# A graph network with experts: joint norms in the first expert network, and a quad's sums cut to the nodes of each tile

## Chip, cores and metric

One core of a Trainium2 chip. The metric is the device time of the whole kernel in microseconds; TensorE, VectorE (DVE in the profile), ScalarE (ACT), GpSimd (POOL) and SyncE (SP, which here only issues transfers) work side by side and are ordered by semaphores.

## What is computed

The reference has 6250 nodes of 256 features and 206,250 edges, sorted by their destination. Everything is f32. Four stages, each added to its input `x`:

```python
# 1: first graph layer, 8 relations
msg = h[edge_src] * edge_norm[:, None]          # h = layernorm(x)
agg = segment_sum(msg, edge_rel * N + edge_dst)  # per relation and destination
out = einsum('rnbi,rbio->nbo', agg, W)           # block-diagonal weights
# 2: first expert network: 2 of 8 experts (512 hidden), the same two for all nodes
h = gelu(xf @ W1[e] + b1[e]); y = h @ W2[e] + b2[e]
out = layer_norm(sum_of_weighted_y + x, gamma, beta)
# 3: graph attention, 8 heads: softmax over the edges of each destination
# 4: second expert network, 8 experts of 256, gated per node
```

## The kernel before, in words

**First graph stage (`gnn0`, from 101 to 2112 us).** The edges lie in 1612 tiles of 128; four tiles are a quad (403 of them), 16 tiles a batch. POOL gathers the source rows of each tile by an indirect transfer (L840) into a ring of 64 tiles; it may run on when TensorE has summed the quad that lay there (`summed`). As edges are sorted, a quad touches few destinations: `NEAR` = 20 nodes from its first. VectorE makes a one-hot of each tile (`one_hots`, L1133) with 20 nodes times 8 relations = 160 columns, weighted by the edge; TensorE multiplies the gathered rows by it (`quad`, L1016), which sums the four tiles of a quad in one PSUM bank; each product is two instructions for each of the two feature halves. VectorE adds the bank to the cells of the batch (L1160), TensorE applies the relation weights (`weigh_one`, L999) and VectorE adds the window to the node sums (L1152). For the second graph stage the edges of the first 96 tiles are also counted by source and node (`pair_hots`, L1225, and `count`, L1056). Between, finished pairs of node tiles get their residual and norm (`norm`), and hidden layers of every second pair of the next network are computed ahead for all eight experts (`look_ahead`, L1067) and stored. `PARTS` says which of the 20 nodes each tile of a quad covers: before, all of them for all four. At the start, `edge_tables` derives from the data a flag, `k.narrow`, whether every tile lies within its part (L551 to L598); if not, all engines take a slower general path.

**First expert network (`ffn0`, 2128 to 2538 us).** 49 node tiles go in 25 pairs, the last of a single tile. `pair_steps` runs step s on every engine, each in its own program order, and a step works on several pairs:

- TensorE: the hidden layer of pair s (L1650; absent for even s below 20, whose hidden layer was computed ahead), interleaved with the output layer of pair s-1 (L1669, eight units of four instructions) and the projection of pair s-3 (L1692), one tile after output unit 0 and the other after unit 5; then the transposes of pair s-2 (`turn`, L1680).
- VectorE: the norm of pair s-2's output (`norm_output`: statistics L1415, aggregates L1419, variance L1421, inverse root by an integer guess and three Newton steps L194 to L199, then L1766 and L1773), `scores` of pair s-3's first tile (L1798 to L1801), the norm of the new rows of pair s-2 (`norm_rows`: statistics, aggregates and root again, then L1786), scores of the second tile, and the adds that take pair s-1's output from PSUM (`add`, L1758). The adds release TensorE's two output banks.
- POOL: waits for the finished rows (`row_done`) of pair s-3, then the residual of pair s (L1617, L1622) and beta of pair s-1 (L1628).
- SP: the ahead-computed hidden layer (L1576), the input of pair s+1 (L1551), and the stores of pair s-2's result (L1555) and pair s-3's table rows (L1564).
- ScalarE: gelu of each hidden unit (L1720), the copy of the transposes (L1726), the exponential for the scores (L1731).

Steps 0 to 3 are written out, 4 to 19 run in a loop, the rest is written out, up to step 27. The output bank of a projection is single: its second tile waits for the scores of the first (`p_moved`), its first for the scores of the second tile before.

**Second graph stage and network (`gnn1_ffn1`, from 2544 us).** It gathers rows of the table that `ffn0` stored (L2083) after a barrier; the change does not touch it.

## Time and profile before

| | |
|---|---|
| median of 3 runs | 4540.59 us (4539.41 to 4543.26) |
| profiled execution, its own time | 4537.89 us |
| its span, first to last instruction | 4535.9 us |
| mean granted TensorE clock | 0.918 of full |
| busy: TensorE, VectorE, ScalarE, POOL | 3594.7, 1875.2, 1064.4, 3081.6 us |
| gathers, first stage: first, last ends | 59.9, 2090.1 us |
| shift L194 beside POOL's add / alone | 1.07 / 0.17 us |
| two aggregates, L1419 | 0.25 us |

The span is what the trace covers, and times inside it count from its start. A profile line gives engine, source line, operation, written tile <- read tiles, count; in brackets the idle time of the engine before it and what ended it. A `PE` line is a matmul, `PEld` its weight load; overlapping instructions are counted once in busy time.

### The profile page before, as it was taken

To read this page: it belongs to the slowest core of one execution; us is meant where nothing else is said; L and a number is where in the kernel's file an instruction comes from. 1 tells how busy PE (TensorE), PEld (TensorE's weight loads), DVE (VectorE), ACT (ScalarE), POOL (GpSimd) and SP (SyncE) were. 2 spreads that over 40 slices of the span, in tenths; PEclk is the share of its full clock that TensorE was granted. 3 is DMA by queue.
4 is the path that set the end of the run, shared out by engine and by line. 5 is a ranking of instruction groups with operands and counts; after the bars stand their busy time and mean duration, and the time that the engine had idled before them with its cause. 6 is when DMAs were issued, how large, how long until landed. Compare 5 with 4: busy or idle time off the path is not lost. (4 is left out here: it accounts for less than half of the span.)

```text
span 4535.9 us, 68376 instructions
## 1 busy us (share of the span) xinstructions
PE 3594.7 (79%) x20702; PEld 3091.2 (68%) x20702; DVE 1875.2 (41%) x6475; ACT 1064.4 (23%) x2405; POOL 3081.6 (68%) x3233
## 2 busy tenths in 40 slices
PE   1777887888888888875889778888887878787788
PEld 1766777777777777774778666666666666666667
DVE  6644545455454544543777412222222222222222
ACT  3001111111111111111335112222222222222223
POOL 4777777777777777773222477777777777777771
PEclk7889999999998999997999888998899999999989
DMA  6344555555555555554221664444444444444441
GB/s 201 109 118 126 171 168 175 175 162 178 168 169 174 171 169 172 170 170 133 80 92 60 209 184 124 124 127 124 126 125 127 125 127 125 128 124 127 123 127 43
DMA packets 302410, 638.19 MB, mean 141 GB/s; under 512 B 66947, under 2 KB 142143, under 8 KB 302192
## 3 DMA queue, kind: packets, MB, share of 16 engines
q0 software_dynamic: 150672, 417.16, 32.6%
q1 hardware_dynamic: 80584, 142.91, 9.8%
q10 hardware_dynamic: 70936, 75.36, 5.1%
q8 instruction: 119, 1.95, 0.2%
q14 instruction: 99, 0.81, 0.1%
HBM read 534.13 MB, written 101.06 MB: 140 GB/s over the span
## 5 line engine op out<-in xcount | busy, mean ns | idle before, releaser
L840 POOL DMA_INDIRECT ring<-xn,index x1588 | 1505.1, 948 | 488.7 <-issue 474.0
L2083 POOL DMA_INDIRECT ring<-table,index x1516 | 1442.9, 952 | 483.4 <-issue 454.8
L1016 PE MATMUL bank<-spare,ring 128*128 128x160 f32 x6448 | 1196.5, 328 | 408.3 <-DMA ring<-xn,index 363.3
L1016 PEld LDWEIGHTS bank<-spare,ring 128*128 128x128 f32 x6448 | 1043.2, 211 | 475.3 <-issue 314.0
L1160 DVE TENSOR_TENSOR spare<-spare,bank 128x320 f32 x403 | 196.7, 488 | 957.4 <-PE bank L1016 932.2
L2405 PE MATMUL bank<-ring,acc 128*32 128x264 f32 x3032 | 292.4, 524 | 335.1 <-DMA ring<-table,index 333.6
L2184 ACT ACTIVATE ework<-bank,bn 128x256 f32<-128x256 f32 x800 | 407.8, 560 | 560.9 <-PE bank L2427 379.0
L1133 DVE TENSOR_SCALAR spare<-cell,scal 128x160 f32<-128x160 f32 x1612 | 510.9, 378 | 0.7 <-ACT scal L856 0.7
L905 ACT ACTIVATE fore_hid<-bank,fore_b 128x256 f32<-128x256 f32 x320 | 151.5, 473 | 1294.5 <-PE bank L1067 1169.8
L2405 PEld LDWEIGHTS bank<-ring,acc 128*32 128x32 f32 x3032 | 139.0, 140 | 451.3 <-issue 432.2
L2427 PE MATMUL bank<-acc,e_w 128*128 (+1 forms) x1600 | 397.4, 395 | 4.9 <-ACT acc L2175 1.7
L2605 DVE TENSOR_TENSOR acc<-cell,off 128x512 f32<-128x512 f32 x102 | 70.7, 693 | 753.2 <-PE bank L2415 729.4
L2440 PE MATMUL bank<-ework,e_w 128*128 128x256 f32 x1600 | 378.1, 379 | 0.0
L2452 PE MATMUL bank<-wo,ework 128*128 128x256 f32 x1600 | 377.9, 379 | 0.0
L2427 PEld LDWEIGHTS bank<-acc,e_w 128*128 128x128 f32 x1600 | 306.3, 197 | 98.3 <-issue 57.0
L1067 PE MATMUL bank<-acc,fore_w 128*128 x1280 | 344.0, 393 | 0.0
L2440 PEld LDWEIGHTS bank<-ework,e_w 128*128 128x128 f32 x1600 | 304.7, 190 | 42.0
L999 PE MATMUL bank<-spare,wblk 128*128 128x140 f32 x1632 | 330.4, 286 | 0.4 <-DVE spare L1160 0.4
L2452 PEld LDWEIGHTS bank<-wo,ework 128*128 128x128 f32 x1600 | 302.7, 190 | 39.5
L2680 DVE SCALAR_TENSOR_TENSOR y<-bank,gate,y 128x256 f32 (+1 forms) x400 | 175.0, 479 | 271.0 <-PE bank L2452 245.0
L999 PEld LDWEIGHTS bank<-spare,wblk 128*128 128x128 f32 x1632 | 270.2, 194 | 0.6 <-DVE spare L1160 0.6
L1067 PEld LDWEIGHTS bank<-acc,fore_w 128*128 128x128 f32 x1280 | 239.4, 203 | 19.2
(338 smaller groups left out, 3118.7 us busy)
## 6 DMA issues: line engine op xcount, KB each, us to landing
fore_w<-in_L_ffn_W SPq DMA_DIRECT2D x82, 512.0 KB, 5.7
fore<-fore_hid SPq DMA_DIRECT2D x80, 512.0 KB
ring<-xn,index POOLq DMA_INDIRECT x1612, 2.8
ring<-table,index POOLq DMA_INDIRECT x1516, 2.8
sums<-acc ACTq DMA_DIRECT2D x101, 132.0 KB, 2.2
hid<-fore SPq DMA_DIRECT2D x20, 512.0 KB, 4.5
counts<-panel ACTq DMA_DIRECT2D x72, 140.0 KB
table<-frow SPq DMA_DIRECT2D x24, 264.0 KB, 3.1
```

The source lines that it names most:

```text
L840: pool.indirect_dma_start(ring[:, m * BT + t, :], None, k.xn_d, bass.IndirectOffsetOnAxis(ap=index[m][:, t:t + 1], axis=0)).then_inc(got[m ...
L999: return pe.matmul(window_ps[:, h, :], k.wblk[:, h, r, :], cells[sums_of(m)][:, i, :], start=(r == 0), stop=(r == RELS - 1))
L1016: ins = pe.matmul(part_of(t, win[q][:, h, :]), ring[:, m * BT + q * QUAD + t, h * P:(h + 1) * P], part_of(t, onehot[:, (q * QUAD + t) % HE ...
L1067: ins = pe.matmul(fore_ps, fore_w[:, e % 2, h, c * P:(c + 1) * P], k.acc[:, h, cols(first_row(fore_group(a)), PCOLS)], start=(h == 0), sto ...
L1133: ins = dve.tensor_scalar(part_of(t % QUAD, onehot[:, t % HELD, :]), part_of(t % QUAD, k.cell[:]), scal[m][:, OFF_KIND, t:t + 1], scal[m][ ...
L1160: dve.tensor_tensor(here, here, win[q].rearrange("p h (r n) -> p (h r) n", n=NEAR), ALU.add).then_inc(added, 1)
L2083: pool.indirect_dma_start(ring[:, par * BT + t, :], None, k.table1_d, bass.IndirectOffsetOnAxis(ap=index[par][:, t:t + 1], axis=0)).then_i ...
L2184: ins = act.activation(dst[:, e % 2, c, :], src[e % 2][:, c, :], ACT.Relu, scale=bn[:, i, q:q + 1], bias=bn[:, i + 1, q:q + 1])
L2405: ins = pe.matmul(win[q * SLICE:(q + 1) * SLICE, :], onehot[:, par * BT + t, :], ring[:, tile_at(par, t), :], start=(u == 0), stop=(u == Q ...
L2427: ins = pe.matmul(p1[e % 2][:, c, :], wa[:, e, h, c * P:(c + 1) * P], xt[:, cols(j % 2 * H + h, 1), :].rearrange("p a n -> p (a n)"), star ...
L2440: ins = pe.matmul(p2[e % 2][:, c, :], wb[:, e, h, c * P:(c + 1) * P], h1[:, e % 2, h, :], start=(h == 0), stop=(h == CH - 1))
L2452: ins = pe.matmul(py[e % 2][:, t * D:(t + 1) * D], h2[:, e % 2, h, t * P:(t + 1) * P], wo[:, e, h, :], start=(h == 0), stop=(h == CH - 1))
```

## The change

`PARTS` becomes ((0, 8), (2, 12), (6, 16), (8, 20)): the four tiles of a quad cover nodes 0 to 7, 2 to 11, 6 to 15 and 8 to 19. All users of `PARTS` follow: one-hots and sums take 64, 80, 80 and 96 columns instead of 160, the counts 56, 70, 70 and 84 instead of 140 per group of blocks, and the flag's bounds are these. In `ffn0` one `statistics` call per step takes the statistics of pair s-2's output and of pair s-3's rows, with one aggregate, variance and root chain on up to four columns. Then come the scores of pair s-4, the row norm of pair s-3, the output norm of pair s-2, the other scores of pair s-4, and the adds of pair s-1. Transposes follow pair s-3, projections, exponentials and scores pair s-4, and one step more is run at the end. Steps 0 to 5 are written out instead of 0 to 3.

```diff
--- before.py
+++ after.py
@@ -74,7 +74,7 @@
 AHEAD0 = P - FIRST0
 NEAR = 20
 CELLS = NEAR * RELS
-PARTS = ((0, NEAR),) * QUAD
+PARTS = ((0, 8), (2, 12), (6, 16), (8, NEAR))
 WINDOW = 140
 PAIRED = 2 * QUADS
 CHUNK_X = 10
@@ -1446,14 +1446,14 @@
 
 
 
-    first, last = 4, 2 * FORE
+    first, last = 6, 2 * FORE
     assert first % 2 == 0 and last % 2 == 0 and last < PAIRS - 1
     for s in range(first):
         step(s, s % 2, s // 2)
     with eng.Fori(first // 2, last // 2) as i:
         step(2 * i, 0, i)
         step(2 * i + 1, 1, i)
-    for s in range(last, PAIRS + 3):
+    for s in range(last, PAIRS + 4):
         step(s, s % 2, s // 2)
 
 
@@ -1523,8 +1523,8 @@
         gamma, beta, b2 = (a.sb(n, [P, D]) for n in ("gamma", "beta", "b2_all"))
         wp = a.sb("wp", [P, H, ROW1])
         ln = Named()
-        ln.stats, ln.mv = a.sb("fstats", [P, PAIR, 6]), a.sb("fmv", [P, PAIR, 2])
-        ln.var, ln.rstd, ln.tmp = (a.sb(f"f{n}", [P, PAIR]) for n in ("var", "rstd", "tmp"))
+        ln.stats, ln.mv = a.sb("fstats", [P, 2 * PAIR, 6]), a.sb("fmv", [P, 2 * PAIR, 2])
+        ln.var, ln.rstd, ln.tmp = (a.sb(f"f{n}", [P, 2 * PAIR]) for n in ("var", "rstd", "tmp"))
         h_ps = [a.bank(f"fh_ps{i}", PCOLS) for i in range(BANKS)]
         y_ps = [a.bank(f"fy_ps{i}", D) for i in range(PAIR)]
         t_ps = a.bank("ft_ps", H * PAIR, P)
@@ -1584,8 +1584,8 @@
                     load(s + 1, 1 - par)
                 if is_pair(s - 2):
                     store_x2(s - 2, par)
-                if is_pair(s - 3):
-                    store_rows(s - 3, 1 - par)
+                if is_pair(s - 4):
+                    store_rows(s - 4, par)
                 if isinstance(s, int) and s == PAIRS - 2:
                     load_piece()
             _, which = nc.values_load_multi_w_load_instructions(
@@ -1629,8 +1629,8 @@
                                    ).then_inc(x1b_made, 1)
 
             def step(s, par, half):
-                if is_pair(s - 3):
-                    pool.wait_ge(row_done, PAIR * (s - 3) + tiles_of_pair(s - 3))
+                if is_pair(s - 4):
+                    pool.wait_ge(row_done, PAIR * (s - 4) + tiles_of_pair(s - 4))
                 if is_pair(s):
                     residual(s, par, half)
                 if is_pair(s - 1):
@@ -1706,10 +1706,10 @@
                         hidden(s, par, half, c)
                     if c >= LEAD and is_pair(s - 1):
                         output(s - 1, 1 - par, half - 1 + par, c - LEAD)
-                    if is_pair(s - 3) and ROWS_AT.get(c - LEAD, PAIR) < tiles_of_pair(s - 3):
-                        project(s - 3, ROWS_AT[c - LEAD])
-                if is_pair(s - 2):
-                    turn(s - 2)
+                    if is_pair(s - 4) and ROWS_AT.get(c - LEAD, PAIR) < tiles_of_pair(s - 4):
+                        project(s - 4, ROWS_AT[c - LEAD])
+                if is_pair(s - 3):
+                    turn(s - 3)
             pair_steps(pe, step)
 
         @block.scalar
@@ -1735,10 +1735,10 @@
                 for c in range(C + LEAD):
                     if c < C and is_pair(s) and not looked_ahead(s, par):
                         keep(s, par, half, c)
-                    if is_pair(s - 3) and ROWS_AT.get(c - LEAD, PAIR) < tiles_of_pair(s - 3):
-                        grow(s - 3, ROWS_AT[c - LEAD])
-                if is_pair(s - 2):
-                    keep_turned(s - 2)
+                    if is_pair(s - 4) and ROWS_AT.get(c - LEAD, PAIR) < tiles_of_pair(s - 4):
+                        grow(s - 4, ROWS_AT[c - LEAD])
+                if is_pair(s - 3):
+                    keep_turned(s - 3)
                 if isinstance(s, int) and s == 1:
                     act.wait_ge(b2_made, 1)
                     act.copy(b2[:], p_ps[:, 0:D]).then_inc(b2_kept, 1)
@@ -1748,8 +1748,7 @@
 
         @block.vector
         def _(dve):
-            HALF_STEPS = group_norm_steps(PAIR) + 2 * PAIR
-            NPER, RPER = HALF_STEPS + group_norm_steps(PAIR) + PAIR, 3
+            NORMS, RPER = group_norm_steps(2 * PAIR) + 3 * PAIR, 3
 
             def add(i, par, t):
                 if t == 0:
@@ -1757,11 +1756,35 @@
                 dve.wait_ge(y_made, PAIR * i + t + 1)
                 dve.tensor_tensor(y[:, t, :], y_ps[t], res[:, par, t, :], ALU.add).then_inc(y_added, 1)
 
-            def norm_output(i, par, half):
+            def statistics(st, o, r, par):
+                outs = [(t, y[:, t, :]) for t in range(tiles_of_pair(o))] if is_pair(o) else []
+                rows = [(PAIR + t, x2[:, 1 - par, t, :]) for t in range(tiles_of_pair(r))] if is_pair(r) else []
+                if outs:
+                    dve.wait_ge(y_added, PAIR * o + len(outs))
+                past_waits(dve, k)
+                for at, v in outs + rows:
+                    st.done(dve.bn_stats(ln.stats[:, at, :], v))
+                st.wait()
+                past_waits(dve, k)
+                for at, _ in outs + rows:
+                    st.done(dve.bn_aggr(ln.mv[:, at, :], ln.stats[:, at, :]))
+                st.wait()
+                used = slice(0 if outs else PAIR, (outs + rows)[-1][0] + 1)
+                st.then(dve.tensor_scalar(ln.var[:, used], ln.mv[:, used, 1], LN_EPS, None, ALU.add))
+                inverse_root(dve, st, ln.var[:, used], ln.rstd[:, used], ln.tmp[:, used])
+
+            def norm_rows(st, i, par):
+                if not (isinstance(i, int) and i == 0):
+                    dve.wait_ge(turned, i)
+                for t in range(tiles_of_pair(i)):
+                    at = PAIR + t
+                    st.done(dve.tensor_scalar(xn2[:, t, :], x2[:, par, t, :], ln.mv[:, at, 0:1], ln.rstd[:, at:at + 1],
+                                              ALU.subtract, ALU.mult))
+                st.wait()
+                dve.sem_inc(normed, 1)
+
+            def norm_output(st, i, par, half):
                 n = tiles_of_pair(i)
-                st = Steps(dve, steps, NPER * i, k)
-                dve.wait_ge(y_added, PAIR * i + n)
-                group_norms(dve, st, k, y, ln, [P] * n)
                 for t in range(n):
                     st.done(dve.scalar_tensor_tensor(y[:, t, :], y[:, t, :], ln.mv[:, t, 0:1], gamma[:],
                                                      ALU.subtract, ALU.mult))
@@ -1773,21 +1796,7 @@
                     st.done(dve.scalar_tensor_tensor(x2[:, par, t, :], y[:, t, :], ln.rstd[:, t:t + 1],
                                                      x1b[:, par, t, :], ALU.mult, ALU.add))
                 st.wait()
-                assert n < PAIR or st.n == HALF_STEPS
                 dve.sem_inc(x2_done, 1)
-
-            def norm_rows(i, par):
-                n = tiles_of_pair(i)
-                st = Steps(dve, steps, NPER * i + HALF_STEPS - 2 * (PAIR - n) * 2, k)
-                group_norms(dve, st, k, x2[:, par, :, :], ln, [P] * n)
-                if not (isinstance(i, int) and i == 0):
-                    dve.wait_ge(turned, i)
-                for t in range(n):
-                    st.done(dve.tensor_scalar(xn2[:, t, :], x2[:, par, t, :], ln.mv[:, t, 0:1], ln.rstd[:, t:t + 1],
-                                              ALU.subtract, ALU.mult))
-                st.wait()
-                assert n < PAIR or st.n == NPER - HALF_STEPS
-                dve.sem_inc(normed, 1)
 
             def scores(i, t, par, half):
 
@@ -1807,15 +1816,22 @@
                 dve.sem_inc(row_done, 1)
 
             def step(s, par, half):
-                tiles = tiles_of_pair(s - 3) if is_pair(s - 3) else 0
-                if is_pair(s - 2):
-                    norm_output(s - 2, par, half - 1)
+                o, r, q = s - 2, s - 3, s - 4
+                tiles = tiles_of_pair(q) if is_pair(q) else 0
+                st = Steps(dve, steps, NORMS * o, k)
+                if is_pair(o) or is_pair(r):
+                    statistics(st, o, r, par)
                 if tiles:
-                    scores(s - 3, 0, 1 - par, half - 2 + par)
-                if is_pair(s - 2):
-                    norm_rows(s - 2, par)
+                    scores(q, 0, par, half - 2)
+                if is_pair(r):
+                    norm_rows(st, r, 1 - par)
+                if is_pair(o):
+                    norm_output(st, o, par, half - 1)
+                if st.n and st.n < NORMS:
+                    dve.sem_inc(steps, NORMS - st.n)
+                assert st.n <= NORMS, st.n
                 if tiles > 1:
-                    scores(s - 3, 1, 1 - par, half - 2 + par)
+                    scores(q, 1, par, half - 2)
                 if is_pair(s - 1):
                     for t in range(tiles_of_pair(s - 1)):
                         add(s - 1, 1 - par, t)
```

## Rows read from the trace of the kernel before

**Rows 1.** The page's costliest groups: busy us, mean ns of one, idle before, releaser

```profile
L840 POOL DMA_INDIRECT ring<-xn,index x1588 | 1505.1, 948 | 488.7 <-issue 474.0
...
L2083 POOL DMA_INDIRECT ring<-table,index x1516 | 1442.9, 952 | 483.4 <-issue 454.8
```

**Rows 2.** Windows: stretch, length, busy us (instructions) by engine, clock, DMA share, GB/s

```profile
600.00:800.00 200.00, 164.93 (x1034) 153.24 (x1033) 103.33 (x369) 37.36 (x86) 151.24 (x161) 0.93 0.55 171
...
2352.00:2382.00 30.00, 26.07 (x123) 22.11 (x122) 23.95 (x93) 11.31 (x18) 7.06 (x6) 1.00 0.26 88
...
2472.00:2502.00 30.00, 30.00 (x158) 26.73 (x157) 21.98 (x88) 19.15 (x31) 7.07 (x6) 1.00 0.17 52
...
3400.00:3600.00 200.00, 160.73 (x925) 126.20 (x918) 51.93 (x160) 57.41 (x139) 151.25 (x161) 0.96 0.46 126
```

**Rows 3.** Waits, 400 to 1900 us: total us, times, longest us

```profile
POOL ring L840 <- PE bank L1016: 7.3, 24, 0.3
```

**Rows 4.** Timeline, first graph stage's tail: start us, us, engine, line, operation, idle before

```profile
2089.11 0.94 POOL L840 DMA_INDIRECT ring<-xn,index  x1 [0.30 <-issue]
...
2092.54 4.06 PE L1016 MATMUL bank<-spare,ring 128*128 128x160 f32 x16 [2.34 <-DMA ring<-xn,index]
...
2101.99 0.65 ACT L863 COPY nsums<-acc 128x512 f32<-128x512 f32 x1 [4.81 <-DVE acc L1152]
```

**Rows 5.** Timeline of the network, one step of VectorE

```profile
2281.53 0.76 DVE L1758 TENSOR_TENSOR fy<-fy_ps,fres 128x256 f32<-128x256 f32 x2 [0.42 <-DVE frow L1801]
...
2284.09 1.07 DVE L194 TENSOR_SCALAR ftmp<-fvar 128x2 int32<-128x2 int32 x1
...
2287.16 0.88 DVE L1766 SCALAR_TENSOR_TENSOR fy<-fy,fmv,gamma 128x256 f32<-128x256 f32 x2
...
2289.49 0.23 DVE L1798 TENSOR_SCALAR fraw<-fp_ps,fm 128x8 f32<-128x8 f32 x1 [0.34 <-DVE fx L1773]
...
2290.64 0.75 DVE L1415 BATCH_NORM_STATS2 fstats<-fx 128x6 f32<-128x256 f32 x2 [0.33 <-DVE frow L1801]
...
2294.31 0.74 DVE L1786 TENSOR_SCALAR fxn<-fx,fmv,frstd 128x256 f32<-128x256 f32 x2
...
2296.43 0.75 DVE L1758 TENSOR_TENSOR fy<-fy_ps,fres 128x256 f32<-128x256 f32 x2 [0.34 <-DVE frow L1801]
```

**Rows 6.** Timeline of the network, the same stretch, TensorE and POOL

```profile
2269.27 1.03 PE L1669 MATMUL fy_ps<-w,hid 128*128 128x256 f32 x4
...
2279.69 1.89 PE L1669 MATMUL fy_ps<-w,hid 128*128 128x256 f32 x8
...
2283.88 1.26 POOL L1628 TENSOR_TENSOR fx1b<-fx,beta 128x512 f32<-128x512 f32 x1
...
2290.42 1.52 PE L1692 MATMUL fp_ps<-wp,fxt 128*128 128x264 f32 x4 [1.99 <-DVEq L1805]
...
2291.73 3.26 PE L1669 MATMUL fy_ps<-w,hid 128*128 128x256 f32 x8
...
2295.65 3.62 PE L1650 MATMUL fh_ps<-acc,w 128*128 x16
```

**Rows 7.** Timeline of the network, its start, the ends of steps, its last store

```profile
2172.79 1.12 PE L1680 MATMUL ft_ps<-ident,fxn 128*128 128x128 f32 x4 [5.89 <-DVEq L1790]
...
2192.01 0.75 DVE L1758 TENSOR_TENSOR fy<-fy_ps,fres 128x256 f32<-128x256 f32 x2 [0.68 <-PE fy_ps L1669]
...
2430.70 0.76 DVE L1758 TENSOR_TENSOR fy<-fy_ps,fres 128x256 f32<-128x256 f32 x2 [0.42 <-DVE frow L1801]
...
2494.74 0.76 DVE L1758 TENSOR_TENSOR fy<-fy_ps,fres 128x256 f32<-128x256 f32 x2 [0.33 <-DVE frow L1801]
...
2509.21 0.76 DVE L1758 TENSOR_TENSOR fy<-fy_ps,fres 128x256 f32<-128x256 f32 x2 [0.32 <-DVE frow L1801]
...
2523.01 0.42 DVE L1758 TENSOR_TENSOR fy<-fy_ps,fres 128x256 f32<-128x256 f32 x1 [0.33 <-DVE frow L1801]
...
2537.66 0.31 SPq L1562 DMA_DIRECT2D table<-frow  x1
```

## The prediction

> **What bounds the kernel now.** I read the groups of instructions first, then the windows, the waits, and the timeline of three places. The kernel is a sequence: a graph stage (to 2112 us), an expert network (2128 to 2538 us), then a second graph stage with the second network. The change touches only the first two. In the groups the row gathers of both graph stages are the largest single-engine loads, 948 and 952 ns each [rows 1]. The windows show their pace: 160 or 161 gathers in 200 us, one per 1.25 us, in either graph stage [rows 2]. In the first, TensorE is busy 165 of 200 us, VectorE 103, so both keep up. The waits agree: from 400 to 1900 us POOL stood 7.3 us in 24 pieces of 0.3 us for TensorE, which is its usual pause between gathers [rows 3]. The first stage ends when its gathers end, plus a tail.
>
> The expert network is another case. In the windows VectorE is busy 24 and TensorE 26 of 30 us, neither full [rows 2]. The timeline of one step shows why: the adds of two successive pairs start at 2281.53 and 2296.43, 14.90 us apart, and between them VectorE runs one chain without a real pause [rows 5], while TensorE waits 1.99 us for it [rows 6]. In the last steps, where TensorE computes every hidden layer itself, it is busy 30 of 30 us instead [rows 2].
>
> **The graph part of the change.** Each tile's one-hot, sum and count cover 64 to 96 columns (mean 80) instead of 160. In the steady part the cover is POOL: what TensorE and VectorE save becomes their idle time, so 0 us. If the gathers sped up with a quieter VectorE, there would be a gain; but they take 948 ns beside a VectorE busy 103 of 200 us and 952 ns beside one busy 52 of 200 [rows 1, 2], so I take 0 for that too. The Trainium skill (GPSIMD Engine Reference, Specifications) says that GpSimd's SBUF interface is shared with VectorE's two-port instructions. By that rule shorter one-hots would shorten gathers; by these rows they would not.
>
> The tail: the last gather runs from 2089.11 to 2090.05, the last quad's 16 matmuls from 2092.54 take 4.06 us, at 1.2 GHz after a wait, and the next step of the tail stands at 2101.99 [rows 4]. Half the columns is 2.1 us: gain 1.9. Ends: 0 if weight loads and not columns set the pace; a loss of 5 if the clock stays low through the 5 us that follow. I take 1.9, nearest to the row itself.
>
> The Trainium skill (TensorE: Matmul & The Clock Gate, LDWEIGHTS) gives 128/1.2 = 107 ns for a load of 128 columns, whatever is streamed. That would be 1.7 us for 16, below 2.1 us; the sum would be the same by it.
>
> **The network part.** Now a step normalises pair s-2, then its output rows again for the projection; two chains of statistics, variance and an 11-step root. After the change the row statistics are taken one step later, together with the next pair's, by one chain on four columns.
>
> *VectorE's step.* Removed: from 2290.64 to 2294.31, 3.67 us [rows 5]. Added: two statistics, 0.75 us [rows 5], and two aggregates, 0.25 us, together 1.0. They are hidden: the shift at 2284.09 takes 1.07 us, against the 0.17 of the same line in the second chain, because it ends with POOL's add, which ends at 2283.88 + 1.26 = 2285.14 [rows 5, 6]. The added 1.0 us lies in that stall. With 0.3 us for what is left of it, a step is 14.90 - 3.67 + 0.3 = 11.5 us.
>
> *TensorE's two steps.* Steps alternate: an even one without hidden layer, an odd one with. I count from the start of VectorE's add before an even step. TensorE is through six output units and the first projection 6.9 us later (2290.42 less 1.99 idle) [rows 6]. The second projection needs the first scores: roots end at 2287.16, so 5.6 us after the add, plus 0.3, plus 0.8 for the scores (2289.49 to about 2290.3) = 6.8 [rows 5]. So it goes at 6.9 and not 8.9. Projection 0.9 and 8 output matmuls 1.8 (the full-speed row, 1.89; now they take 3.26 [rows 6]) = 9.6; transposes 0.5 = 10.1; four hidden units 3.4 (3.62 with its fill) = 13.5. VectorE was ready at 11.5, so TensorE decides. From its first output unit to the last an odd step takes 2269.27 to 2281.4, 12.1 us [rows 6]: 25.6, and 0.3 to the add: 25.9 us for two steps against 29.8. Gain 3.9 per two steps. The adds at 2192.01 and 2430.70 enclose 16 such steps [rows 7]: **31.6 us**. Ends: if TensorE never waited, its own work of 25.1 (9.5 + 3.5 + 12.1) gives 38; if its clock falls as now, see the first rival.
>
> *The start.* TensorE waits 5.89 us before the first transposes, at 2172.79, for the second norm, with hidden layers queued behind them [rows 7]. That turn moves a step later, so the hidden units start at 2166.9 instead of 2173.7: 6.8 us, and two projections (1.7) also leave this step: **8.5 us**. Ends 4 and 11.
>
> *The last steps.* Four steps of 16.03 us are TensorE's: 0. Then 2494.74 to 2509.21, 14.47 us [rows 7]: with a short hidden layer TensorE needs 12.9, gain 1.6. Then 2509.21 to 2523.01, 13.8: little POOL stall, so 13.8 - 3.67 + 0.7 = 10.8, gain 3.0.
>
> *The drain.* From the last add at 2523.01 to the last row store at 2537.66 is 14.65 us [rows 7]. With one more stage: statistics of three tiles and root 4.8; scores, row norm and output norm 3.3; the second scores of pair 22 wait for a projection and end at 10.1; the next root chain 3.2 brings 13.4; scores of pair 23 0.9, row norm 0.6, projection, exponential and scores 3.0 bring 17.9; projection and scores of the last tile 3.7: 21.6. **Loss 7.0**; ends 5 and 10.
>
> Moved with it: the row store (SP) and POOL's wait for the finished rows go from pair s-3 to s-4, but both stand at the same scores in the step, so POOL's residual starts as before, and the hidden load, issued some 6 us after the add and landing by 11.5, is wanted at 13.5. Behind POOL's wait stand the residual and beta adds, whose reader comes a step later: 0. The wider tiles cost nothing.
>
> **Sum:** 1.9 + 31.6 + 8.5 + 1.6 + 3.0 - 7.0 = 39.6 us. What follows starts from a barrier and is paced by its own gathers, so it moves as a whole. The profiled execution took 4537.9 us (span 4535.9), so 4498 of its kind; the median of the runs is 4540.6, 2.7 above, so **4501 us**.
>
> **Rivals.**
> *The clock eats the gain (0.12).* Now TensorE's clock drops in the even step after its wait: 8 matmuls take 3.26 us instead of 1.89 [rows 6]. If some wait stays and keeps it low through the four hidden units too, 1.5 + 2.4 us per two steps, 31 of 39.6 us go: 4532. For it: the clock falls there now. Against: the wait shrinks from 1.99 to almost nothing. Halfway it gives 4516.
> *TensorE becomes the bound of the first graph stage (0.02).* Narrower sums make it idler and the chip may hold it at 1.2 GHz. It is busy 4.1 us per quad of four gathers (5.0 us) at a clock of 0.93 [rows 2], some 3.8 of full-speed work; about 1.0 goes, 2.8 stays. At a mean clock below 2.8/5.0 = 0.56 it falls behind POOL; at 0.5 it needs 5.6 us, +0.6 for 403 quads, some 240 us once the ring's slack is used: about 4740. Against: falling behind means being busy without a gap, and such stretches of this trace run at 1.00 [rows 2]. The Trainium skill's clock gate section says the same, that activity releases the throttle.
> *The new order ties both engines worse (0.05).* A joint chain delays the output norm behind scores and row norm, to 10 us after the add instead of 7.6. If POOL or SP, queued on that, came a step late, the gain would shrink to the start and be lost in the drain: -8.5 + 7 - 1.9, about 4537, no change. Against: their readers have a whole step.
> *It doesn't do what it says (under 0.01).* If one tile broke its bounds, the kernel's flag would send all to the general path, far slower. From the reference's dst array: in the 403 quads the tiles start 0, 3 to 5, 6 to 9 and 10 to 13 nodes from the quad's first and end at most at 5, 9, 13 and 18. The parts start at 0, 2, 6, 8 and end before 8, 12, 16, 20. All fit.
>
> **How the numbers follow.** The forecast has 0.80, the clock rival 0.12, the worse tie 0.05, the graph stage 0.02, the general path 0.01. A difference of 0.2% (9 us) is about what a measurement of this kernel can tell from none. Within it lie 0.02 of the clock rival (its full price) and 0.03 of the worse tie: 0.05. Slower are the graph stage 0.02, the general path 0.01 and the rest of the worse tie with a long drain, 0.01: 0.04. Faster: 0.91. The range takes the ends of the forecast's start, loop, drain and tail together, which rarely all fall on one side, and the clock rival's half: a gain of 19 to 52 us, 4488 to 4522.
>
> **What would show it.** In the profile after: gathers still 1.25 us apart and the last one ending near 2090; sum matmuls of 64 to 96 columns, TensorE's busy share in that stage down by some 15 to 25 of 200 us; adds 25.9 us per two steps, VectorE no longer the chain; one root chain per step, on four columns; the shift's stall moved onto the variance add; from last add to last row store near 21.6 us. I am wrong if adds stay over 28 us per two steps, if the transposes or projections still wait 2 us, or if the gathers' end moves.

## The result, and the profile after

The changed kernel takes 4500.32 us (median of 6 runs, 4498.5 to 4504.32) against 4540.67 us: ratio 0.9912, 95% interval 0.9899 to 0.9925, 40 us faster where 39.6 were forecast. The profiled execution took 4503.21 us (span 4501.4), so it lies 2.9 us above its median, where that of before lay 2.8 below; per stretch the two traces are therefore the better measure. One of the twelve executions of `parts_only`, a kernel below, took 14,033 us and is left out of its figures; it left no trace, and its cause is open.

| stretch | before | after | difference | forecast |
|---|---|---|---|---|
| last gather's end | 2090.05 | 2091.20 | +1.2 | 0 |
| from there to the second add of pair 0 | 69.98 | 71.72 | +1.7 | -1.9 |
| pair 0's add to pair 2's (start) | 31.98 | 20.38 | -11.6 | -8.5 |
| 16 steps, pair 2 to 18 | 238.69 | 207.26 | -31.4 | -31.6 |
| pair 18 to 22 | 64.04 | 64.04 | 0.0 | 0 |
| pair 22 to 23, 23 to 24 | 14.47, 13.80 | 12.70, 10.44 | -1.8, -3.4 | -1.6, -3.0 |
| last add to last row store | 14.65 | 20.57 | +5.9 | +7.0 |
| first gather of the last stage starts | 2545.55 | 2506.16 | -39.4 | -39.6 |

Adds are counted by their start; where a pair's two adds run together that is the first one's, 0.34 us before the second's. Of after, pair 2's adds stand apart (2180.70 and 2183.64), and 2183.30 is taken.

The page's groups of after: the gathers of either stage are as they were [rows 1]; the sums (L1016) on half the columns are busy 108 us less, and the weight matmuls (L999), which weren't changed, 58 us more.

```profile
L840 POOL DMA_INDIRECT ring<-xn,index x1588 | 1506.3, 949 | 488.6 <-issue 479.2
L2099 POOL DMA_INDIRECT ring<-table,index x1516 | 1446.1, 954 | 489.3 <-issue 454.2
L1016 PE MATMUL bank<-spare,ring 128*128 128x80 f32 (+2 forms) x6448 | 1088.4, 317 | 418.8 <-DMA ring<-xn,index 367.2
...
L1133 DVE TENSOR_SCALAR spare<-cell,scal 128x64 f32<-128x64 f32 (+1 forms) x1612 | 418.2, 335 | 0.4 <-ACT scal L856 0.4
...
L999 PE MATMUL bank<-spare,wblk 128*128 128x140 f32 x1632 | 388.2, 324 | 0.4 <-DVE spare L1160 0.4
```

The same two groups of before:

```profile
L1016 PE MATMUL bank<-spare,ring 128*128 128x160 f32 x6448 | 1196.5, 328 | 408.3 <-DMA ring<-xn,index 363.3
...
L999 PE MATMUL bank<-spare,wblk 128*128 128x140 f32 x1632 | 330.4, 286 | 0.4 <-DVE spare L1160 0.4
```

Windows of after, columns as in [rows 2]: still 160 gathers in 200 us, TensorE's clock 0.85 where it was 0.93. In the network TensorE is busy 29.7 of 30 us, VectorE 22.

```profile
600.00:800.00 200.00, 156.43 (x1001) 143.49 (x1001) 88.14 (x359) 35.95 (x85) 151.27 (x160) 0.85 0.55 171
...
2352.00:2382.00 30.00, 29.70 (x140) 25.52 (x139) 21.95 (x85) 14.91 (x24) 9.03 (x8) 1.00 0.28 92
```

Waits of after, 400 to 1900 us, the row that answers to [rows 3]:

```profile
POOL ring L840 <- PE bank L1016: 3.3, 11, 0.3
```

Timeline of after, the first stage's tail, against [rows 4]. The last quad's 16 matmuls take 3.70 us on 64 to 96 columns (the row names the first shape), at a granted clock of 0.50; 16 at full clock, a little earlier, 1.92. The 32 weight matmuls behind them (L999) take 5.38 us, at a clock of 0.74 from 2098 to 2103; before, they took 4.08 at full clock.

```profile
2084.79 1.92 PE L1016 MATMUL bank<-spare,ring 128*128 128x64 f32 x16
...
2090.25 0.95 POOL L840 DMA_INDIRECT ring<-xn,index  x1 [0.30 <-issue]
2093.53 3.70 PE L1016 MATMUL bank<-spare,ring 128*128 128x64 f32 x16 [3.47 <-DMA ring<-xn,index]
...
2097.91 5.38 PE L999 MATMUL bank<-spare,wblk 128*128 128x140 f32 x32 [0.44 <-DVE spare L1160]
...
2103.93 0.65 ACT L863 COPY nsums<-acc 128x512 f32<-128x512 f32 x1 [6.15 <-DVE acc L1152]
```

Of before, 16 matmuls on 160 columns at full clock, two quads ahead of the last:

```profile
2082.69 2.34 PE L1016 MATMUL bank<-spare,ring 128*128 128x160 f32 x16
```

Timeline of after, VectorE in an even step (no hidden layer), with POOL's beta add, against [rows 5]: four statistics, four aggregates, one root. The adds are 11.58 us apart. The shift (L194) takes 0.17 us now. The stall beside POOL stands at the variance add (L1773, 0.78): it ends at 2290.27, POOL's add at 2290.24.

```profile
2286.62 0.76 DVE L1757 TENSOR_TENSOR fy<-fy_ps,fres 128x256 f32<-128x256 f32 x2 [0.42 <-DVE frow L1810]
...
2288.19 0.73 DVE L1766 BATCH_NORM_STATS2 fstats<-fx 128x6 f32<-128x256 f32 x2
2288.97 1.27 POOL L1628 TENSOR_TENSOR fx1b<-fx,beta 128x512 f32<-128x512 f32 x1
2289.07 0.38 DVE L1770 BATCH_NORM_AGGREGATE fmv<-fstats 128x2 f32<-128x6 f32 x4
2289.49 0.78 DVE L1773 TENSOR_SCALAR fvar<-fmv 128x4 f32<-128x4 f32 x1
2290.41 0.17 DVE L194 TENSOR_SCALAR ftmp<-fvar 128x4 int32<-128x4 int32 x1
...
2292.81 0.23 DVE L1807 TENSOR_SCALAR fraw<-fp_ps,fm 128x8 f32<-128x8 f32 x1 [0.25 <-DVE frstd L199]
...
2298.20 0.42 DVE L1757 TENSOR_TENSOR fy<-fy_ps,fres 128x256 f32<-128x256 f32 x1 [0.34 <-DVE frow L1810]
```

The same stretch on TensorE, against [rows 6]: the wait before the second projection is 0.22 us instead of 1.99, the eight matmuls behind it take 1.89 us, and the transposes (L1680) follow without a wait.

```profile
2293.74 1.16 PE L1692 MATMUL fp_ps<-wp,fxt 128*128 128x264 f32 x4 [0.22 <-DVEq L1814]
2294.74 1.89 PE L1669 MATMUL fy_ps<-w,hid 128*128 128x256 f32 x8
2296.46 0.60 PE L1680 MATMUL ft_ps<-ident,fxn 128*128 128x128 f32 x4
2296.90 3.62 PE L1650 MATMUL fh_ps<-acc,w 128*128 x16
2300.36 1.03 PE L1669 MATMUL fy_ps<-w,hid 128*128 128x256 f32 x4
```

The step of before in [rows 6], whose eight matmuls took 3.26 us, isn't typical. Only two of the loop's eight even steps look like it (from 2291.73 and 2410.96); in the other six the eight matmuls ran at full clock too, and TensorE then waited once more, 1.85 us at the transposes, for VectorE's row norm (L1790 of before). Two stretches later in the trace of before:

```profile
2320.25 1.16 PE L1692 MATMUL fp_ps<-wp,fxt 128*128 128x264 f32 x4 [1.99 <-DVEq L1805]
2321.24 1.89 PE L1669 MATMUL fy_ps<-w,hid 128*128 128x256 f32 x8
2324.98 0.66 PE L1680 MATMUL ft_ps<-ident,fxn 128*128 128x128 f32 x4 [1.85 <-DVEq L1790]
```

So TensorE waited some 3.85 us in such an even step, and waits 0.22 now: 3.6 of the 3.9 us that two steps gained. The low clock cost nothing before; those two steps, 14.90 and 14.92 us between adds, were no longer than the rest.

The end of the network, on SP's queue and POOL, against [rows 7] for the store: the last add, at 2477.74, is 20.57 us ahead of the last row store.

```profile
2498.31 0.31 SPq L1562 DMA_DIRECT2D table<-frow  x1
...
2506.16 0.98 POOL L2099 DMA_INDIRECT ring<-table,index  x1 [27.79 <-ACT index L2115]
```

### The profile page after: what moved, and what is told of

It is laid out like the page before. It is cut to its first block and busy times, and to the rows that moved or that the text cites. A ratio compares the mean times of both kernels' runs of the same rounds, so it can differ in the third digit from the quotient of the medians.

```text
span 4501.4 us, 67684 instructions
## 1 busy us (share of the span) xinstructions
PE 3580.6 (80%) x20702; PEld 3067.6 (68%) x20702; DVE 1693.9 (38%) x6187; ACT 1057.9 (24%) x2403; POOL 3086.4 (69%) x3233
## 5 line engine op out<-in xcount | busy, mean ns | idle before, releaser
L1016 PE MATMUL bank<-spare,ring 128*128 128x80 f32 (+2 forms) x6448 | 1088.4, 317 | 418.8 <-DMA ring<-xn,index 367.2
L1016 PEld LDWEIGHTS bank<-spare,ring 128*128 128x128 f32 x6448 | 1040.2, 236 | 492.5 <-issue 354.1
L1133 DVE TENSOR_SCALAR spare<-cell,scal 128x64 f32<-128x64 f32 (+1 forms) x1612 | 418.2, 335 | 0.4 <-ACT scal L856 0.4
L1067 PE MATMUL bank<-acc,fore_w 128*128 x1280 | 409.4, 451 | 1.4 <-ACT fore_hid L905 1.4
L999 PE MATMUL bank<-spare,wblk 128*128 128x140 f32 x1632 | 388.2, 324 | 0.4 <-DVE spare L1160 0.4
L1067 PEld LDWEIGHTS bank<-acc,fore_w 128*128 128x128 f32 x1280 | 264.4, 229 | 28.9 <-ACT fore_hid L905 1.6
L999 PEld LDWEIGHTS bank<-spare,wblk 128*128 128x128 f32 x1632 | 271.9, 210 | 0.6 <-DVE spare L1160 0.6
```

Source lines behind the costliest of these rows:

```text
L999: return pe.matmul(window_ps[:, h, :], k.wblk[:, h, r, :], cells[sums_of(m)][:, i, :], start=(r == 0), stop=(r == RELS - 1))
L1016: ins = pe.matmul(part_of(t, win[q][:, h, :]), ring[:, m * BT + q * QUAD + t, h * P:(h + 1) * P], part_of(t, onehot[:, (q * QUAD + t) % HE ...
L1067: ins = pe.matmul(fore_ps, fore_w[:, e % 2, h, c * P:(c + 1) * P], k.acc[:, h, cols(first_row(fore_group(a)), PCOLS)], start=(h == 0), sto ...
L1133: ins = dve.tensor_scalar(part_of(t % QUAD, onehot[:, t % HELD, :]), part_of(t % QUAD, k.cell[:]), scal[m][:, OFF_KIND, t:t + 1], scal[m][ ...
```

## The experiments

**Each half of the change alone.** Four kernels ran beside each other (the fourth, `two_chains`, comes next), against a median of 4548.99 us for the kernel before on that chip. `again` is the changed kernel; `joint_only` and `parts_only` differ from the changed kernel and from the kernel before by one line:

```diff
# joint_only, from after
-PARTS = ((0, 8), (2, 12), (6, 16), (8, NEAR))
+PARTS = ((0, NEAR),) * QUAD
# parts_only, from before
-PARTS = ((0, NEAR),) * QUAD
+PARTS = ((0, 8), (2, 12), (6, 16), (8, NEAR))
```

> The changed kernel once more, as the yardstick of this call. Both theories: 0.991 of the kernel before, some 4500 us, adds of the expert network 25.9 to 26.0 us apart per two steps, first gather of the last stage near 2506.

> The network part of the change alone, PARTS as before. If all the gain is the network's and the narrower parts cost the first graph stage's tail 1.8 us and the load behind it 1.1 us, as the two traces show: the second add of pair 0 back at 2160.0, the first gather of the last stage near 2503 to 2504, and 2 to 3 us faster than the changed kernel, 4497 to 4498. The rival, that the narrower parts bring something that the traces hide (shorter gathers under a quieter VectorE): slower than the changed kernel by some us, 4503 or more. If the last stage's 4.9 us more of the changed kernel were the parts' doing and no scatter between executions, it goes too: 4493.

> The graph part of the change alone, the network as before. Cover theory: POOL's gathers decide, so the last gather still ends at 2090 to 2091 and TensorE's clock in that stage falls to about 0.84; the network's adds stay 29.8 us apart per two steps; total 0 to 3 us above the kernel before, 4540 to 4544. The rival (VectorE and GpSimd share an interface, so shorter one-hots let gathers run faster): last gather earlier by more than 5 us and a total below 4536.

`again`: 4509.15 us, ratio 0.9913 (0.9898 to 0.9927), adds 25.98 us per two steps; first gather of the last stage at 2508.02. `joint_only`: 4506.85 us, 0.9909 (0.9895 to 0.9923), second add of pair 0 at 2163.64 and first gather at 2506.84, each 1.2 earlier than `again`. The positions were foretold too early, since on this chip the last gather ended some 3 us later in each (2094.53, 2093.97). The medians differ by 2.3 us, as expected; but of the 3 us foretold between the positions only 1.2 came, and 0.6 of them is the earlier last gather. `parts_only`: 4553.14 us, 1.0008 (0.9999 to 1.0017), adds 29.84 us per two steps, clock 0.861 over the run; its last gather ended at 2094.40, no earlier than the others'. The whole gain is the network's; the parts bring none. Whether they cost 2 us of the total isn't settled by these medians.

**One chain, or only a deeper pipeline?** `two_chains` keeps everything the change moved a step later, but computes the two norms by two chains again:

```diff
# in step(); `statistics` itself now takes the tiles and the wait
-                if is_pair(o) or is_pair(r):
-                    statistics(st, o, r, par)
+                if is_pair(o):
+                    statistics(st, [(t, y[:, t, :]) for t in range(tiles_of_pair(o))], PAIR * o + tiles_of_pair(o))
                 if tiles:
                     scores(q, 0, par, half - 2)
                 if is_pair(r):
+                    statistics(st, [(PAIR + t, x2[:, 1 - par, t, :]) for t in range(tiles_of_pair(r))], None)
                     norm_rows(st, r, 1 - par)
```

> The changed kernel with its later transposes, projections and scores kept, but with the statistics, variance and root of the output and of the rows as two separate chains again, the second after the first scores. Theory A (VectorE's second chain was what bounded a step): the loop is back at about 29.5 to 30 us per two steps, the gain of 31 us in the loop is gone, the start keeps most of its 11 us, the drain is longer by 6 to 12 us; total 4535 to 4550. Rival B (what gained is that transposes and projections stand a step later, so that TensorE never waits for fresh norms): 26 us per two steps stays and the total is 4500 to 4508.

It took 4550.6 us, 1.0003 (0.9994 to 1.0012), 0.6 us above the range expected; its two steps take 30.03 us, where 29.5 to 30 were. Its timeline of VectorE shows the second chain back, from 2284.11 to 2287.87 (3.76 us, where [rows 5] had 3.67), and adds 15.04 us apart:

```profile
2277.09 0.76 DVE L1757 TENSOR_TENSOR fy<-fy_ps,fres 128x256 f32<-128x256 f32 x2 [0.42 <-DVE frow L1808]
...
2284.11 0.75 DVE L1764 BATCH_NORM_STATS2 fstats<-fx 128x6 f32<-128x256 f32 x2 [0.33 <-DVE frow L1808]
...
2287.87 0.74 DVE L1779 TENSOR_SCALAR fxn<-fx,fmv,frstd 128x256 f32<-128x256 f32 x2
...
2292.13 0.75 DVE L1757 TENSOR_TENSOR fy<-fy_ps,fres 128x256 f32<-128x256 f32 x2 [0.34 <-DVE frow L1808]
```

The 16 steps take 238.61 us, as before the change (238.69); the start keeps 10.4 of its 11.6 us; the drain is 23.95 us, 9.3 longer than before. So the later staging alone wins the start and gives it back at the end. The loop's 31 us need the joint chain, which in turn needs the later staging. Theory A holds, B falls.

**Which engine sets a step.** Four kernels, beside a median of 4541.23 us for the kernel before. Two take a Newton round from each root (VectorE, 0.59 us per chain), two leave out an output unit (TensorE, four matmul instructions; the network's output lacks that part of its sum). The first edit is shown in short, the count of rounds being an argument in the kernels:

```diff
 # before_two_rounds, after_two_rounds: in the expert network's roots
-    for _ in range(3):
+    for _ in range(2):
 # before_seven, after_seven: in output()
-                if t >= tiles_of_pair(i):
+                if t >= tiles_of_pair(i) or u == 2:
                     return
```

> The kernel before, with two instead of three Newton rounds in both root chains of the expert network (the roots are less exact; nothing else changes). Three instructions of about 0.2 us leave each of the two chains of a step. Theory A (VectorE's chain bounds the step before): each step shorter by 2 x 0.59 = 1.2 us, so 27.5 us per two steps instead of 29.8, some 19 us in the 16-step loop and 22 to 26 us in all, 4515 to 4519 where the kernel before takes 4541. Rival B (TensorE's wait for a late norm is what bounds): also shorter, but only by the first chain's 0.6 us per step, since the second chain lies behind the projection: 10 to 14 us.

> The changed kernel with two instead of three Newton rounds (less exact roots). Its one chain per step is 0.6 us shorter. Theory A (TensorE bounds the changed loop): 25.9 to 26.0 us per two steps stay as they are, and only the start, the last steps and the drain, where VectorE is waited for, give 3 to 5 us. If VectorE still bounded every step, 0.6 x 24 steps plus the drain's, 15 to 18 us.

> The kernel before without one of the eight output units of a step (the third unit of the first tile, four instructions, 0.93 to 1.0 us of TensorE; that part of the second product is left out). Theory A: TensorE waits for VectorE in that kernel, so the adds stay 29.8 us per two steps; only the four steps of 16.03 us, which are TensorE's, give 0.9 each: 3 to 5 us in all. If TensorE bounded every step: some 22 us.

> The changed kernel without the same output unit. Theory A: TensorE bounds it, so two steps take 1.9 us less, 24.0 instead of 25.9 (VectorE's floor is 11.5 per step, 23.0), and with the four TensorE steps the whole gives 18 to 22 us. If VectorE's joint chain bounds it: under 6 us.

| kernel | us, ratio (95%) | even step, odd step | 16 steps |
|---|---|---|---|
| before (trace above) | | 14.91, 14.92 | 238.69 |
| before_two_rounds | 4526.18, 0.9967 (0.9956 to 0.9978) | 13.73, 14.93 | 229.49 |
| before_seven | 4534.60, 0.9985 (0.9976 to 0.9995) | 14.92, 14.87 | 238.37 |
| after (trace above) | | 11.58, 14.40 | 207.26 |
| after_two_rounds | 4497.27, 0.9901 (0.9884 to 0.9917) | 11.00, 14.50 | 203.94 |
| after_seven | 4487.02, 0.9879 (0.9863 to 0.9896) | 11.58, 13.53 | 199.97 |

Each of the four expectations missed in part: `before_two_rounds` gained 15 us, not 22 to 26; `before_seven` kept its adds at 29.8, but gained 6.6 us, not 3 to 5 (1.9 at the start, 4.3 in the four TensorE steps); `after_two_rounds` gained 4.7 us from pair 0's add to the first gather of the last stage, within the 3 to 5 expected, but 3.3 of them in the loop, where none was foretold; `after_seven` gained 14 us against the other runs of the changed kernel, not 18 to 22. The path isn't one engine's.

In the kernel before, a shorter VectorE chain shortens only the even step (by 1.2 us, as priced), and less TensorE work shortens the 16 steps by 0.3 us in all. Both engines' paths were 14.9 us long in the odd step: VectorE's own chain (14.87 with a TensorE unit less), and TensorE from the transposes on (14.93 with shorter chains). With the chains 1.2 us shorter VectorE stands in the odd step, waiting for the second projection's exponential, which TensorE reaches no sooner. In `before_two_rounds` (timeline of VectorE, then of TensorE):

```profile
2303.45 0.23 DVE L1798 TENSOR_SCALAR fraw<-fp_ps,fm 128x8 f32<-128x8 f32 x1 [1.38 <-ACT fgrown L1731]
```

```profile
2313.01 1.16 PE L1692 MATMUL fp_ps<-wp,fxt 128*128 128x264 f32 x4 [1.41 <-DVEq L1805]
...
2317.16 0.66 PE L1680 MATMUL ft_ps<-ident,fxn 128*128 128x128 f32 x4 [1.26 <-DVEq L1790]
```

The second of these rows is the link, the same wait as at 2324.98 above and 0.6 us shorter: the transposes wait for the row norm (L1790), and TensorE's hidden layer is queued behind them. So rival B was right that TensorE's waits matter, but wrong on the first chain alone: both chains of the even step lie ahead of the row norm, and the step lost 1.2 us, not 0.6. The total of 15 us lies between what A and B said.

In the changed kernel a TensorE unit less shortens the odd step by 0.87 and the even step not at all. `after_seven` and `after_two_rounds`, the same instruction in each:

```profile
2286.97 1.16 PE L1692 MATMUL fp_ps<-wp,fxt 128*128 128x264 f32 x4 [1.08 <-DVEq L1814]
```

```profile
2291.31 1.05 PE L1692 MATMUL fp_ps<-wp,fxt 128*128 128x264 f32 x4
```

With a unit less ahead of it, the second projection of the even step waits 1.08 us for the first scores instead of 0.22: the unit's 0.86 us became a wait. With a shorter root it doesn't wait at all, and the two steps take 25.50 us, against 25.98. So the changed kernel's path runs from the even step's add through VectorE's joint chain and first scores (7.1 us), then through TensorE (18.9 us) to the next even add. TensorE alone takes 25.5; the chain is 0.5 us too long for it. Hence 8 x 0.48 = 3.8 us are to be had in the loop from a shorter root, of which 3.3 were measured. Of `after_seven`'s 14 us the trace places 13.4: 7.3 in the loop's odd steps, where the removed unit stands behind that link, 3.5 in the four TensorE steps and 2.6 at start and end.

**What the parts do to the first stage.** Beside a median of 4539.09 us for the kernel before, the changed kernel and the network part once more, and two hybrids. `wide_hots` lets VectorE fill all 160 columns while TensorE multiplies the part; in `wide_sums` TensorE multiplies all 160 while VectorE fills the part:

```diff
 # wide_hots
-dve.tensor_scalar(part_of(t % QUAD, onehot[:, t % HELD, :]), part_of(t % QUAD, k.cell[:]),
+dve.tensor_scalar(onehot[:, t % HELD, :], k.cell[:],
 # wide_sums, with the one-hot buffers cleared once
-ins = pe.matmul(part_of(t, win[q][:, h, :]), ring[:, m * BT + q * QUAD + t, h * P:(h + 1) * P],
-                part_of(t, onehot[:, (q * QUAD + t) % HELD, :]), start=(t == 0),
+ins = pe.matmul(win[q][:, h, :], ring[:, m * BT + q * QUAD + t, h * P:(h + 1) * P],
+                onehot[:, (q * QUAD + t) % HELD, :], start=(t == 0),
```

> The changed kernel as the yardstick of this call: 0.991 of the kernel before; TensorE's granted clock 0.82 to 0.84 in the first graph stage; the last gather's end to the route's first reduction about 24.5 us.

> The network part alone once more: 1 to 3 us faster than the changed kernel (2.3 in the first comparison), clock 0.93 in the first graph stage.

> The changed kernel, but VectorE makes each one-hot on all 160 columns; TensorE still multiplies only the part. Theory: what the parts cost, 2 us, comes from TensorE, which idles more and is granted 0.83 instead of 0.93, so that the matmuls of the stage's tail run at half clock. Then this kernel keeps clock 0.83 and the time of the changed kernel within 1 us. Rival: a VectorE with other timing moves POOL's gathers: then it takes the time of the network part alone.

> The changed kernel, but TensorE multiplies all 160 columns of each tile, while VectorE fills only the part (the rest of the buffers is cleared once at the start, under 1 us more). Theory: TensorE is as busy as before, the clock is back at 0.93, the tail is as in the network part alone, and the time is 1 to 3 us below the changed kernel. Rival: time of the changed kernel, clock back without any gain.

| kernel | us, ratio (95%) | granted clock, 600 to 1600 us | L999 x32 in the tail, us | last gather's end to pair 0's second add |
|---|---|---|---|---|
| again2 | 4499.33, 0.9915 (0.9901 to 0.9928) | 0.83 | 6.72 | 72.2 |
| joint_only2 | 4500.14, 0.9916 (0.9902 to 0.9929) | 0.92 | 4.08 | 68.4 |
| wide_hots | 4500.93, 0.9919 (0.9905 to 0.9932) | 0.83 | 6.76 | 71.9 |
| wide_sums | 4496.95, 0.9907 (0.9892 to 0.9922) | 0.92 | 4.37 | 70.1 |

The windows from 600 to 800 us, first of `wide_hots`, then of `wide_sums`, columns as in [rows 2]:

```profile
600.00:800.00 200.00, 162.51 (x1019) 149.53 (x1019) 101.21 (x365) 36.94 (x86) 151.25 (x161) 0.84 0.55 171
```

```profile
600.00:800.00 200.00, 162.54 (x995) 152.35 (x994) 87.87 (x359) 35.85 (x85) 151.36 (x160) 0.90 0.55 171
```

The clock goes with TensorE's sums and not with VectorE's one-hots: with narrow sums it is 0.83 beside either one-hots, with wide sums 0.92. `again2` missed one expectation: from the last gather's end to the route's first reduction (L1359) it took 25.8 us, not 24.5. In the tail the weight matmuls (L999) show the clock most plainly. First `wide_hots`, then `wide_sums`:

```profile
2092.10 3.70 PE L1016 MATMUL bank<-spare,ring 128*128 128x64 f32 x16 [3.12 <-DMA ring<-xn,index]
...
2096.48 6.76 PE L999 MATMUL bank<-spare,wblk 128*128 128x140 f32 x32 [0.45 <-DVE spare L1160]
```

```profile
2091.89 3.39 PE L1016 MATMUL bank<-spare,ring 128*128 128x160 f32 x16 [3.17 <-DMA ring<-xn,index]
...
2095.96 4.37 PE L999 MATMUL bank<-spare,wblk 128*128 128x140 f32 x32 [0.45 <-DVE spare L1160]
```

In all twelve traces whose output layer is complete, from the last gather's end to pair 0's second add, the kernels with wide sums take 69.98, 69.67, 68.35, 70.06 and 70.1 us (mean 69.6), those with narrow ones 71.72, 70.29, 72.04, 71.7, 72.2, 71.93 and 71.79 (mean 71.7). That is the parts' cost: 2 us on average, though `wide_sums` (70.1) and the fastest narrow trace (70.29) all but touch. The totals can't resolve it, and the expectations set on them were too fine: the network part alone against the changed kernel was -2.3 us in one comparison and +0.8 in the other, `wide_hots` +1.6 where within 1 was expected. `wide_sums` has the lowest median of the four, 2.4 us below the changed kernel, and that too is unresolved. So no run here shows a version that beats the changed kernel beyond doubt.

## Why the prediction was right, and where it wasn't

- **Graph part, steady state: 0.** Right. The last gather ended within 1.3 us for the four kernels of the last group (2089.35 to 2090.59), at 947 to 948 ns per gather, with VectorE busy 88 or 101 of 200 us. The Trainium skill (GPSIMD Engine Reference, Specifications) says that GpSimd's SBUF interfaces are shared with VectorE, by which shorter one-hots might have made gathers shorter; the trace doesn't show that for these instructions. It does show VectorE held by POOL elsewhere: a small instruction of VectorE ends with POOL's add, the shift before (at 2285.16, the add at 2285.14 [rows 5, 6]) and the variance add now (2290.27 and 2290.24).
- **Tail: -1.9 forecast, +1.7 measured**, 2 on average over the twelve traces. The wrong step is "half the columns is 2.1 us". The 16 matmuls took 3.70 instead of 4.06. At full clock 16 narrow ones take 1.92 us and 16 wide ones 2.34 (two quads from the end, in the trace of before): even there halving the columns gives 0.4. Something else than the columns sets the pace of narrow sums. That it is the weight loads, which I had held as an end, priced at 0, is likely, but no run takes the loads away. The Trainium skill (TensorE: Matmul & The Clock Gate, LDWEIGHTS) gives 128/1.2 = 107 ns per load, by which I estimate 1.7 us for 16; that fits the 1.92 at full clock. At 1.2 GHz the same 16 take 3.70, about twice, so its figure can't be used at that level, as I did when I wrote that it gave 1.7 us here. The other end, "a loss of 5 if the clock stays low", came in part: L999 took 5.4 to 6.8 us in the traces with narrow sums, 4.1 before.
- **TensorE's busy share in that stage, down by 15 to 25 of 200 us:** wrong, 164.93 to 156.43 in this window and 820 to 798 of 1000 over a longer one. Shorter sums saved 108 us (L1016, 1196.5 to 1088.4), and at the lower clock L999 and the computed-ahead layer (L1067) took 58 and 65 us more. It cost nothing, because POOL covers it.
- **VectorE's step: 11.5 forecast, 11.58 measured**, with the stall moved as described.
- **TensorE's two steps: 25.9 forecast, 25.98 measured**, 31.6 against 31.4 us for the loop. But "TensorE decides" is only mostly true: the second projection was to go 6.9 us after the add, as TensorE allowed and with VectorE 0.1 ahead; it goes at 7.12, and VectorE's first scores hold it. The wait of 0.22 us and the pause around it make the two steps 0.48 us longer than the 25.50 of `after_two_rounds`, where TensorE doesn't wait. Forecast 25.6, plus 0.3 to the add: near by sum, not by its parts.
- **Start: -8.5 forecast, -11.6 measured**, just outside its ends of 4 and 11. The row before named only the transposes' wait of 5.89 us and two projections. The adds show two pieces: from pair 0 to 1 4.6 us less, where VectorE no longer runs the second chain ahead of pair 1's add, and from pair 1 to 2 7.0 less, near the 6.8 of the moved wait. The first piece I had not counted beyond two projections.
- **Last steps: -1.6 and -3.0 forecast, -1.8 and -3.4 measured. Drain: +7.0 forecast, +5.9 measured.**
- **Errors that cancel.** The start was 3.1 us and the drain 1.1 us better than forecast; the tail 3.6 us and the last gather 1.2 worse. The total's agreement within 1 us is partly luck; the loop's isn't.
- **Rivals.** The clock rival fell: the wait shrank to 0.22 us and the matmuls behind it run at full speed. Its ground was weaker than I thought: I took "TensorE's clock drops in the even step" from one step, and six of the eight even steps before ran at full clock. The second wait of 1.85 us in those six I had missed; the forecast came out even so, because it built TensorE's new step from its work and not from its old waits. The graph stage didn't become TensorE's: POOL's waits for it fell from 7.3 to 3.3 us even at 0.85 of the clock. The worse tie didn't show: in the loop TensorE waited for nothing but the first scores, 1.3 us in all.
- **The last stage "moves as a whole":** from its first gather to the end it took 1990.4 before and 1995.2 after. Executions of the changed kernel alone gave 1995.2, 1998.0 and 1991.3, those with other parts or chains 1987.7 to 1999.2, so 4.8 us is within the scatter. By it the two profiled executions differ by only 34.5 us in span, while the medians, of six executions each, differ by 40.

## What to carry to other kernels

When two engines hand a pipeline back and forth, "which engine bounds" can be the wrong question: here neither did alone. Remove a little from each, in the model or on the chip, and see which step shrinks. And look at more than one period of a loop before building on a row: the step shown before the change was one of two that differed from the other six. Joining two short dependent chains into one pays by the fixed cost of its instructions (eleven tiny ones of 0.2 us here), and needs a stage of delay that is paid once, at the drain. Narrower matmuls with full 128x128 weights saved little here (0.4 of 2.34 us per quad at full clock), and they cost clock for what ran beside and behind them.

## What was not expected of the hardware

- 16 matmuls with 128x128 weights took 1.92 us on 64 to 96 columns, 2.34 on 160, both at full clock; 3.70 and 4.06 in the tail at the low one.
- Half the columns in the sums lowered the granted clock of the stage from 0.92 to 0.84 (0.83 in the runs after it), and instructions that weren't changed got slower: L999 from 286 to 324 ns, L1067 from 393 to 451 ns on average.
- The stall of VectorE beside POOL's adds hit two small tensor-scalar instructions (the shift with 1.07 us instead of 0.17 before, the variance add with 0.78 after), not the statistics and aggregates that ran ahead of them beside the same adds (0.73 and 0.38 us).
